# Blocks of nodes cut by step instead of by chunk, and their edges counted a group ahead, in a graph layer followed by an LSTM

## The reference

```python
# x: 3125 nodes x 256; src, dst: 53125 edges, sorted by dst
def layernorm(x): return (x - mean(x)) / sqrt(var(x) + 1e-5)

h   = layernorm(x) @ weight + bias
agg = segment_sum(h[src], dst, 3125);  deg = max(number of edges of dst, 1)
x   = x + agg / deg

xt = layernorm(x)                      # a sequence of 3125 steps
xi, xf, xg, xo = xt @ U_i + b_i, xt @ U_f + b_f, xt @ U_c + b_c, xt @ U_o + b_o
for t in range(3125):                  # h, c start at 0; f_t is not used
    i, g, o = sigmoid(xi[t] + h @ V_i), tanh(xg[t] + h @ V_c), sigmoid(xo[t] + h @ V_o)
    c = h * c + i * g
    h = o * tanh(c)
    hs[t] = h
x = x + hs
```

## Time and profile before

| | us |
|---|---|
| median of three runs (544.05 to 546.68) | 545.43 |
| the profiled execution | 543.02 |
| its span, first to last instruction | 541.2 |

### The profile page before, as it was taken

How to read it: one execution, slowest core, us unless ns; L and a number is a source line. 1 busy time by engine, 2 the same in 40 slices (tenths; PEclk the granted TensorE clock), 3 DMA queues, 4 the chain that set the end, 5 groups by cost and what they waited for, 6 DMA issues and landing times.

```text
span 541.2 us, 15807 instructions
## 1 busy us (share of the span) xinstructions
PE 430.0 (79%) x6225; PEld 373.5 (69%) x6225; DVE 389.5 (72%) x1135; ACT 361.0 (67%) x967; POOL 217.5 (40%) x415
## 2 busy tenths in 40 slices
PE   1079885987998999999999998955777778788880
PEld 1046663876887889888988896744666767677770
DVE  1487888688777777877778784447677768888883
ACT  0145644564567768777767775678788988888880
POOL 3323502345324434525434543413345554444540
PEclk9987876999999999999999999975699999999996
DMA  3563003310100010001000000123000000110111
GB/s 106 163 177 81 0 2 98 103 39 2 49 1 2 1 49 2 2 1 49 3 2 19 30 1 1 33 112 134 12 3 3 2 5 2 50 34 20 50 51 54
DMA packets 15185, 21.00 MB, mean 39 GB/s; under 512 B 2284, under 2 KB 14004, under 8 KB 14979
## 3 DMA queue, kind: packets, MB, share of 16 engines
q1 hardware_dynamic: 12208, 16.78, 9.4%
q0 software_dynamic: 1440, 1.71, 1.2%
q10 hardware_dynamic: 1456, 1.42, 0.8%
HBM read 10.28 MB, written 9.61 MB: 37 GB/s over the span
## 4 chain that ended last, share of the span: by engine, by line
PE 50%; DVE 21%; ACT 13%; issue 6%; POOL 4%; DMA 3%; SPq 1%; DVEq 0%; ACTq 0%
PE bank L1032 9%; PE bank L1034 9%; PE bank L1147 9%; PE bank L1063 9%; PE bank L1103 5%; DVE ig L1586 4%; DVE c_st L1592 4%; PE bank L1021 4%; ACT gate L892 4%; DVE h L1597 3%; ACT tc L906 3%; DMA x_sb<-in_x_dram 3%; ACT gx L786 3%; PE bank L1080 2%; DVE hots L1520 2%
## 5 line engine op out<-in xcount | busy, mean ns | idle before, releaser
L1032 PE MATMUL bank<-h_flat,counts 125*128 125x257 f16 x625 | 170.6, 275 | 0.0
L1034 PE MATMUL bank<-h_flat,counts 125*128 125x256 f16 x625 | 168.7, 272 | 0.0
L1147 PE MATMUL bank<-h,V 128*128 128x63 f16 (+1 forms) x3216 | 116.2, 196 | 43.7 <-DVE h L1597 38.8
L840 ACT ACTIVATE counts<-bank 125x500 f16<-125x500 f32 (+1 forms) x175 | 97.4, 557 | 79.0 <-PE bank L1103 77.6
L1147 PEld LDWEIGHTS bank<-h,V 128*128 128x128 f16 x3216 | 107.4, 100 | 55.6 <-issue 40.9
L1103 PE MATMUL bank<-hots 128*128 128x125 f16 x625 | 136.2, 224 | 7.2 <-DVE hots L1520 7.0
L1520 DVE TENSOR_TENSOR hots<-iota,kp 128x1024 f16<-128x1024 f16 x157 | 105.0, 699 | 2.4 <-ACT kp L829 1.9
L626 POOL TENSOR_SCALAR newton<-rstd,var_eps 125x1 f32<-125x1 f32 x50 | 43.7, 874 | 123.7 <-DVE rstd L1478 121.2
L1103 PEld LDWEIGHTS bank<-hots 128*128 128x128 f16 x625 | 60.1, 98 | 18.2 <-DVE hots L1520 6.6
L1032 PEld LDWEIGHTS bank<-h_flat,counts 125*128 125x128 f16 x625 | 61.6, 98 | 7.3 <-ACT counts L840 0.2
L1063 PE MATMUL bank<-z2T,U 128*128 128x250 f16 (+1 forms) x540 | 57.1, 256 | 11.0 <-DVE z2T L1490 6.2
(11 more groups left out here) (153 smaller groups left out, 652.1 us busy)
## 6 DMA issues: line engine op xcount, KB each, us to landing
h_dram<-h_flat SPq DMA_DIRECT2D x1, 3137.2 KB
x_dram<-x_sb SPq DMA_DIRECT2D x25, 125.0 KB
x_sb<-x_dram SPq DMA_DIRECT2D x1, 3125.0 KB
out_dram<-x_sb SPq DMA_DIRECT2D x4, 625.0 KB
x_sb<-in_x_dram SPq DMA_DIRECT2D x17, 125.0 KB
x_sb<-in_x_dram ACTq DMA_DIRECT2D x8, 125.0 KB
out_dram<-x_sb SPq DMA_DIRECT2D x1, 375.0 KB
gx<-in_L_gnn_weight_dram ACTq DMA_DIRECT2D x1, 256.0 KB, 4.7
```

The costliest lines, as they stand in the source:

```text
L840: nc.scalar.activation(counts[:, j % 2, :, n0:n0 + n], ps_count[group % 3][0:NB, 0:n * BLOCKS].rearrange("p (n s) -> p s n", n=n), ACT.Cop ...
L1032: nc.tensor.matmul(ps_sum[turn % 2][:, 0:D + 1], counts[:, turn % 2, s, :], line[:, s, D:2 * D + 1], start=(s == 0), stop=False, skip_grou ...
L1034: return nc.tensor.matmul(ps_sum[turn % 2][:, 0:D], counts[:, turn % 2, s, :], line[:, s, 0:D], start=False, stop=(s == BLOCKS - 1), skip_ ...
L1147: mm = nc.tensor.matmul(to[:, (m - m0) * n:(m - m0 + 1) * n], V16[:, v_part, d, m * P:(m + 1) * P], h16[:, h_part, d, c0:c1], start=False, ...
```

## The change

A block is now one step of all 125 chunks. `x` comes by five transfers of five steps, three on SP and two on ACT, and `x1` is stored by five and not loaded back, since its layout in `x_sb` is that of the output. An edge's place in its block is its chunk, and its key is worked out with seven operations on 125 x 640 elements instead of 17; they stand at `j` = 11 to 14 instead of 18 to 24, and the turn and the copy into `kp` at `j` = 15. The windows are 125 to a group of five blocks (before 25 to a block). The counts of a group stand in one of two buffers of five blocks, so the first 125 windows are counted before the sums start: 24 groups of one-hots are made inside the loop of the first normalization, two to a `j` from 17 on, the others behind it. The list has 670 places; at place `w` PE counts window `w + 125` and adds to the sum number `w - 4`. `gx` is cut by steps, and needs for turn `t` only block `t`: `HIDDEN` is 25, turn `t` begins at place `(t + 3) * 25 + 14`, and turns 21 to 25 at the places in `LAST_TURNS`. The gates take blocks in pairs, eleven pairs and three single ones (before, ten pairs and five single ones). DVE's maxima over the weights (L1300) stand at places 6 and 12, behind the start of the sums' list.

```diff
-HIDDEN = 20
+HIDDEN = 25
-    NW = BLOCKS * WINDOWS
+    NW = GROUPS_S * WINDOWS
-    ORDER = [RUN * k + s for s in ORDER_S for k in range(RUN)]
+    ORDER = [RUN * s + r for s in ORDER_S for r in range(RUN)]
-        counts_all = sb("counts", [P, 2, BLOCKS, P], F16)
-        counts = counts_all[0:NB, :, :, :]
+        counts_all = sb("counts", [P, RUN, BLOCKS, P], F16)
+        counts = [counts_all[0:NB, :, :, :],
+                  gx_flat[0:NB, COUNTS_AT:COUNTS_AT + COUNTS_LEN].bitcast(F16).rearrange(
+                      "p (r t n) -> p r t n", r=RUN, t=BLOCKS)]
-        SUM_AFTER = WINDOWS + 3
-        FINISH_AT, NORM_AT, TURN_AT, HIGH_AT, LOW_AT = (17, 2), (10, 3), (8, 3), (12, 3), (1, 4)
+        SUM_AFTER = 4
+        FINISH_AT, NORM_AT, TURN_AT, HIGH_AT, LOW_AT = 35, 53, 59, 63, 67
+        LAST_AT = {FINISH_AT: (583, 605, 630), NORM_AT: (598, 616, 640), TURN_AT: (603, 618, 641),
+                   HIGH_AT: (606, 620, 642), LOW_AT: (609, 622, 643)}
+        PAIRS = 11
+        LAST_GATES = {PAIRS: (614, 617, 620), PAIRS + 1: (625, 628, 631), PAIRS + 2: (645, 646, 647)}
+        LAST_PARTS = {E_SEED: 0, E_PRODUCTS: 1, E_GATE: 2, E_CELL: 3, E_OUT: 4, E_OUT_GATE: 5, E_TANH: 6, E_STATE: 8}
+        LAST_TURNS = {21: 612, 22: 621, 23: 631, 24: 641, 25: 651}
+        KEYS_FROM, TURN_KEYS, HOTS_FROM = 11, 15, 17
+        HOTS_AHEAD = 3
+        def first_hots(j):
+            return range(max(0, 2 * (j - HOTS_FROM)), max(0, 2 * (j - HOTS_FROM + 1)))
...
@@ sync
-            for c in range(BLOCKS // X_CHUNK):
-                for r in range(3 if c < X_SHARED else RUN):
-                    sp.dma_start(x_sb[parts(r), js, :], x_rows[c, r, :, :, :]).then_inc(x_in[c], 16)
+            for c in range(0, BLOCKS // X_CHUNK, 2):
+                sp.dma_start(x_sb[:, js, :], x_steps[:, js, :]).then_inc(x_in[c], 16)
-            sp.wait_ge(z2_ready, BLOCKS)
-            load_x1()
@@ gpsimd
-            weights_top(1, 0, 1)
             pool.wait_ge(rows_known, 1)
             for b in range(WIN_BATCHES):
                 pool.indirect_dma_start(
...
+                if b == 0:
+                    weights_top(1, 0, 1)
-            for j in range(2, BLOCKS + 4):
-                if 1 <= j - 3 - RUN <= HIDDEN:
-                    early_old_part(j - 3 - RUN)
-                if j - 2 < BLOCKS:
-                    root(j - 2, ORDER[j - 2])
+            for j in range(1, HIDDEN + 4):
+                if 1 <= j - 3 <= HIDDEN:
+                    early_old_part(j - 3)
+                if j - 1 < BLOCKS:
+                    root(j - 1, ORDER[j - 1])
@@ scalar
+            def counts_out(w):
...
+                act.wait_ge(count_ps, w + 1)
+                if i == HOT_WINDOWS - 1 and g >= 2:
+                    act.wait_ge(sum_ps, RUN * (g - 1))
+                nc.scalar.activation(counts[g % 2][:, :, :, n0:n0 + n],
+                                     ps_count[group % 3][0:NB, 0:n * KEYS].rearrange(
+                                         "p (n r t) -> p r t n", n=n, r=RUN),
+                                     ACT.Copy).then_inc(counted, 1)
@@ tensor, inside the loop over j of the first normalization
+                if j == TURN_KEYS:
+                    turn_keys()
+                for k in first_hots(j - 1):
+                    for w in range(HOT_WINDOWS * k, HOT_WINDOWS * (k + 1)):
+                        count(w)
@@ tensor, the places
+            for w in range(PLACES_END):
+                if w + WINDOWS < NW:
+                    count(w + WINDOWS)
...
+                t, s = divmod(w - SUM_AFTER, BLOCKS)
+                if 0 <= t < BLOCKS:
+                    if s == 0:
+                        if t % RUN == 0:
+                            pe.wait_ge(counted, (t // RUN + 1) * OUTS)
```

More of the change, by code:

```diff
@@ L20 @@
 RUN = 5
-WINDOWS = 25
+WINDOWS = 125
 HOT_WINDOWS = 4
@@ L393, in block_at @@
+        FINISH_AT, NORM_AT, TURN_AT, HIGH_AT, LOW_AT = 35, 53, 59, 63, 67
+        GATES_AT = 71
+        LAST_AT = {FINISH_AT: (583, 605, 630), NORM_AT: (598, 616, 640), TURN_AT: (603, 618, 641),
+                   HIGH_AT: (606, 620, 642), LOW_AT: (609, 622, 643)}
+        PLACES_END = 670
+        def block_at(w, place):
             last = LAST_AT[place]
[L394 to L397 removed]
+            if w in last:
+                return BLOCKS - len(last) + last.index(w)
+            b, rest = divmod(w - place, BLOCKS)
+            return b if rest == 0 and 0 <= b < BLOCKS - len(last) else None
@@ L999, in _, with turn_keys, count @@
             mm.then_inc(before_ps, 1)
+            def turn_keys():
+                pe.wait_ge(edges_placed, 2)
+                for a, of in ((PART, edge_chunk), (KEY, edge_key)):
+                    for b in range(WIN_BATCHES):
+                        mm = nc.tensor.transpose(edges_at(a, b), of[:, b, :], ident[0:WIN_ROWS, 0:WIN_ROWS])
+                mm.then_inc(edges_ps, 1)
+            def count(w):
+                group, pos, _ = out_group(w)
+                if w == 0:
+                    pe.wait_ge(keys_ready, 6)
+                if w % HOT_WINDOWS == 0:
+                    pe.wait_ge(hot_ready, w // HOT_WINDOWS + 1)
+                if pos == 0 and group >= 3:
+                    pe.wait_ge(counted, group - 2)
+                ring, g = w // HOT_WINDOWS % RING, w % HOT_WINDOWS
+                nc.tensor.matmul(ps_count[group % 3][:, pos * KEYS:(pos + 1) * KEYS],
+                                 hots[:, ring, 0, g // 2, :, g % 2], hots[:, ring, 1, g // 2, 0:KEYS, g % 2],
+                                 start=True, stop=True).then_inc(count_ps, 1)
             for j in range(BLOCKS + 2):
@@ new lines, in _ @@
+            for w in range(PLACES_END):
+                if w + WINDOWS < NW:
+                    count(w + WINDOWS)
+                if w == 113:
+                    pe.wait_ge(uv_split, 6)
+                    nc.tensor.matmul(ps_early[:, 0:2 * HH * CHUNKS], V16[:, 0, 0, 0:P],
+                                     V16[:, 0, 0, 0:2 * HH * CHUNKS], start=True, stop=True).then_inc(bits_early, 1)
+                t = early_turn(w, E_PRODUCTS)
+                if t:
+                    early_products(t, 0, 2 * HH)
+                t = early_turn(w, E_OUT)
+                if t:
+                    early_products(t, 2 * HH, MT)
+                for b, (j0, j1), u in gates_at(w):
+                    gates_x(j1 - j0, b % 2, j1)
+                t, s = divmod(w - SUM_AFTER, BLOCKS)
[3 more added lines that the diff above has]
+                            pe.wait_ge(counted, (t // RUN + 1) * OUTS)
+                        if t == 0:
+                            pe.wait_ge(line_ready, BLOCKS)
+                        if t >= 2:
+                            pe.wait_ge(x1_ready, t - 1)
+                    mm = sums(t, s)
+                    if s == BLOCKS - 1:
+                        mm.then_inc(sum_ps, 1)
+                t = block_at(w, TURN_AT)
+                if t is not None:
+                    turn_z2(t)
+                if t == BLOCKS - 1:
+                    pe.wait_ge(counted, GROUPS_S * OUTS)
+                    pe.wait_ge(x1_ready, BLOCKS)
+                    set_bits()
@@ L1283, in floor_of @@
                 rounded(to)
-            def places(node, win, chunk, part):
-                floor_of(win, node, RUN)
-                floor_of(chunk, win, RUN)
-                floor_of(part, chunk, ROWS)
-                for to, by, of in ((node, -float(RUN), win), (win, -float(RUN), chunk), (chunk, -float(ROWS), part),
-                                   (win, float(RUN), part)):
-                    link(nc.vector.scalar_tensor_tensor(out=to, in0=of, scalar=by, in1=to, op0=ALU.mult, op1=ALU.add))
             dve.wait_ge(iotas, 4)
@@ L1418, in _ @@
             scales(0, 1, 6, 1)
+            for k in range(6):
+                chunk_deviation(0, k)
             for j in range(X_CHUNK, 2 * X_CHUNK):
                 chunk_stats(j)
-            for k in range(6):
-                chunk_deviation(0, k)
             chunk_to_root(1)
```

518 lines of the change are left out of this document (222 added, 296 removed).

## The result

The changed kernel takes 552.26 us (median of 4, 550.42 to 554.26), the kernel before 546.05 in the same comparison (544.05 to 546.93): ratio 1.012, 95% interval 1.007 to 1.017. It is slower, by about 6 us, where 540.6 was forecast with a range up to 549. The profiled execution took 550.42 us (543.02 before), with a span of 548.5 (541.2).

What follows compares the result with a forecast made beforehand. PE was taken to set the pace in the sums, with alternating PE and DVE before and dependent small operations in the open turns. 4.5 + 1.7 + 3.3 - 14.3 = -4.8 from 545.43 gave 540.6 us, range 530 to 549.

Steps and rivals of the forecast that it cites:

- a, the start: Up to the first sum: more one-hots on DVE, less edge work and later maxima, +4.5 us.
- Ahead of the first use of the edges, at 33 us, this is hidden but for 1 us: Loads of `x`: the first chunk lands some 3.5 us later; all but 1 us hidden, that inside the +4.5.
- the front absorbs the counts: Rival, before the first sum: idle DVE and PE time takes most one-hots, start +0, 531 to 535 us; chance 0.20.
- The clock rival: Rival, from `j` = 18 to the first sum: PE stays at 1.2 GHz, start +11.5, 547.6 us; chance 0.11.
- b, the sums: First to last sum: fewer counts in the list against more turns, gates and maxima there, +1.7 us.
- waits at the edges of groups: Rival, in the sums: counts complete only four places ahead, 2 us at each of four edges, 548.6 us; chance 0.10.
- The maxima on DVE stand behind the start now: In the sums: maxima in front of one-hots made three groups ahead; half of 3.5 us stays, +1.5.
- c, the tail: Last sum to first open turn: turn 25 now waits for the last block's gates, +3.3 us.
- I add nothing: In the tail: turns 23 and 24 run while block 24's own chain would be waiting, so no time added.
- the other term, -1.3: In the tail: the single block's gates no longer queue behind a pair's on PE and ACT, 1.3 us less.
- d, open turns: Turns in the open: five rough turns fewer at 2.86 us each, -14.3 us.
- the rival of slow copies: Rival, copies of counts: short runs double the 586 ns, +18 us ahead of the sums, +8 in them, 567; chance 0.06.

Runs made afterwards that it cites:

- front_top_first: Changed kernel with GpSimd's maximum over the partitions put back ahead of the five fetches of edge rows: 551.46 us, ratio 1.011.
- front_x_pieces: Changed kernel with `x` loaded by 25 transfers of one step (runs of 1 KB) on the same two queues: 546.67 us, ratio 0.998.
- front_runs1k: Changed kernel with `x` loaded by six large transfers that take every second step, in runs of 1 KB: 550.46 us, ratio 1.007.
- sums_out1: Changed kernel with `x` in 25 loads and ACT taking gates out of PSUM one place behind their products instead of three: 537.68 us, ratio 0.986.
- before_out1: Kernel before the change with ACT taking gates out of PSUM one place behind their products instead of three: 541.48 us, ratio 0.990.
- sums_light: Changed kernel with `x` in 25 loads, first state's memsets at the program's start, three low halves of `V` later: 546.20 us, ratio 0.999.
- tail_hidden20: Changed kernel with `x` in 25 loads and only 20 early turns, the other five in the open: 551.98 us, ratio 1.013.
- tail_pool_order: Changed kernel with the old part of turn 23 ahead of the last block's root on GpSimd: 550.82 us, ratio 1.009.
- after: The changed kernel itself, against the kernel before: 552.26 us, ratio 1.012.

## Why the prediction was wrong

**a, the start, +6.5 for +4.5.** The number is near by luck: a loss of 5.4 us was missed, and the counting was charged 3 us too high. The step that failed is "Ahead of the first use of the edges, at 33 us, this is hidden but for 1 us". I followed the loads of `x` and asked when `x` lands (the first chunk 1.4 us later, the third at 26.8 us for 29.45), but not what else was on the DMA engines at that time. The rows of edges, 1.7 KB each (425 numbers of 4 bytes), fetched beside runs of 5 KB, came at 37.7 us, for a use that DVE was ready for at 28.4. `front_top_first` excludes the order of issue, `front_x_pieces` brings the use back to 33.6 without a wait and the first sum to 92.8. That the runs' length does it, and not the number of loads, is shown by `front_runs1k` (a fetch landed in 8.1 us for 14.6); by what mechanism the DMA engines favour the long runs, no run here shows. What I charged, the counting, is nearly free: in seven kernels with the changed loop and the loads in 25, the first sum stood at 90.4 to 95.6 us, 92.9 in the mean (92.8, 95.6, 90.4, 90.5, 92.4, 94.3, 94.0), against 91.7, so +1.2, with single kernels from -1.3 to +3.9. My rival "the front absorbs the counts" was nearer there.

The working had it wrong at "the last block ends about 7 us later": by the earlier trace rows a block with edge operations took 2.32 us before, and the 2.2 us of a block with one-hots take their place, so these rows give no 7 us. Nor does the reading of the earlier trace rows hold that larger runs were no faster: between 8 and 13 us the changed kernel moved 133 GB/s, `front_x_pieces` 120, and its third chunk of `x` was there at 26.80 us for 31.95.

The Trainium skill's rule to coalesce (DMA: Bandwidth & Descriptors, Rules for kernel authors), which I weighed only as a gain, was a loss in this kernel: five loads instead of 25 cost 5.4 us at the first sum. For `x` alone the traces agree with it in the changed kernel (133 GB/s for 120), but by the longer runs: the six large loads of `front_runs1k`, in runs of 1 KB, moved 121. The clock rival did not come: 0.95 between 50 and 83 us, before 0.84.

**b, the sums, +11.8 for +1.7.** The terms of work were fair: PE's busy time rose by 2.5 us. The step that failed, and the largest of all, is that the sum had no term for PE's waits, though the change set all places anew. I priced "waits at the edges of groups" as a rival, at the counts' end; they were not there (0.3 us at the first sum), but at the gates' bank (12 times) and the seeds (11 times), 8.5 us more than before (8.0 + 6.1 for 4.1 + 1.5). `sums_out1` shows it with one number (264.5 to 252.9), and `before_out1` that by the stretch of the sums most of it came with the change (3.3 us there), with the reserve made above. The order of ACT's list around a unit of gates was to be had before the run: the groups of four counts restarted with each block before, and now run through 125 windows, so that they end at other places in each block of 25, with gates three places behind. That this drift is why the waits grew is my reading; no run changes it alone. The 4.5 us wait for DVE at the first gates was 2.5 in `sums_light`, where the memsets and three low halves were taken away from it; that was worth 2.4 us, and nothing once ACT's order was mended. "The maxima on DVE stand behind the start now", +1.5, was the place, too small; what the maxima themselves cost there was not tried. One term was also added up wrong: the 0.8 us given back for the eleventh pair is not what stands beside it, 36 matmuls at 0.06, which is 2.2.

**c, the tail, +5.1 for +3.3.** The mechanism, turn 25 waiting for the last block's gates, was right, and its 4.6 us too (4.6 between `tail_hidden20` and `front_x_pieces`; `tail_pool_order`: the wait on GpSimd was real, 2.6 us, and worth 0.8). The step that failed is "I add nothing" for turns 23 and 24: they hold up the last block's normalization by 1.9 us and its gates by 2.1. Together the five turns cost 8.6 us in the tail. That the forecast was only 1.8 us off is luck: the other term, -1.3, was too small as well, since with 20 early turns in the new layout the tail is 11.8 us, 3.8 below the 15.6 before.

**d, open turns, -14.1 for -14.3.** Right. Moved the other way, five turns gave 15.9 us from the first turn in the open to the end.

**At nothing.** The copy of the counts took 604 and 595 ns into the two buffers for 586, so the rival of slow copies did not come, and `x1` showed nowhere.

**The chances.** The 0.18 for the same and the 0.18 for slower do not follow from the shares given for them: two thirds of the 0.21 of the clock and the edges are 0.14, not 0.09.

The changed kernel had a gain in it. With loads of 1 KB runs and gates taken out one place behind, it is 1.4% faster than before (`sums_out1`); but the kernel before with its gates taken out so is already 1.0% faster (`before_out1`), which leaves some 3.8 us, where 4.8 were forecast, to the change with its loads mended.

## What to carry to other kernels

When a load is regrouped, look at what else is in flight on the DMA engines at that time and who waits for it, not only at the load's own landing. When a list of places is set anew, write out for each in-order engine what stands ahead of each release that another engine needs: an eviction that is listed behind a copy of work not yet done waits for it, and here that cost 11.6 us, more than the 2.5 us of work that the change added to PE in the sums. Price hidden turns by what they add to the end of the list, not by their work.

## What the runs showed of the hardware

Fetches of rows of 1.7 KB by indirect DMA took 14.6 us from issue to landing beside loads in runs of 5 KB, and 7.7 and 8.1 beside loads in runs of 1 KB, be these 25 or six (medians of the last three fetches, `after`, `front_x_pieces`, `front_runs1k`). Issuing the last fetch 3.2 us earlier beside the 5 KB runs (19.9 for 23.1 us) let the rows be used 0.4 us earlier (37.4 for 37.7). Between 8 and 13 us the loads in 5 KB runs moved 133 GB/s, those in 1 KB runs 120 (25 loads) and 121 (six). GpSimd waited 5.8 to 7.9 us ahead of its first maximum over the partitions, over all fourteen kernels, whether it stood ahead of the first fetch or behind it.
